# A norm at each layer boundary: rows shared by two engines, transposes in another order, a reciprocal root in nine steps, and memsets by words

## The reference

```python
def _layernorm(x, axis=-1, eps=1e-05):
    m = jnp.mean(x, axis=axis, keepdims=True)
    v = jnp.var(x, axis=axis, keepdims=True)
    return (x - m) / jnp.sqrt(v + eps)
...
x = x + _L0_xattn_ref(ctx_1024, _layernorm(x, axis=-1), ...)
x = x + _L0_ffn_ref(_layernorm(x, axis=-1), ...)
x = x + _L1_xattn_ref(_layernorm(x, axis=-1), ctx_1024, ...)
x = x + _L1_ffn_ref(_layernorm(x, axis=-1), ...)
x = x + _L2_xattn_ref(_layernorm(x, axis=-1), ctx_1024, ...)
x = x + _L2_ffn_ref(_layernorm(x, axis=-1), ...)
x = x + _L3_xattn_ref(_layernorm(x, axis=-1), ctx_1024, ...)
x = x + _L3_ffn_ref(_layernorm(x, axis=-1), ...)
```

## Time and profile before

| what | value |
| --- | --- |
| median of 3 runs | 2140.48 us (2140.2 to 2141.39) |
| the profiled execution's own time | 2137.22 us |
| its span in the profile | 2135.4 us |
| PE busy | 1727.2 us (81% of the span) |
| DVE busy | 1149.1 us (54%) |
| ACT busy | 731.7 us (34%) |
| POOL busy | 205.8 us (10%) |
| chain that ended last, by engine | PE 66%, DVE 20%, issue 6%, ACT 6% |

### The profile page before, as it was taken

One profiled execution on the slowest core, in us unless ns is written; L12 is line 12 of the kernel. 1 busy time (PEld: TensorE's weight loads), 2 busy tenths in 40 slices (PEclk: granted clock), 3 DMA queues, 4 the chain that ended last, 5 costly groups with the idle time before them and its releaser, 6 DMA issues.

```text
span 2135.4 us, 26508 instructions
## 1 busy us (share of the span) xinstructions
PE 1727.2 (81%) x8160; PEld 1137.7 (53%) x8160; DVE 1149.1 (54%) x2224; ACT 731.7 (34%) x1757; POOL 205.8 (10%) x307
## 2 busy tenths in 40 slices
PE   3565897478883558898879999997799999969998
PEld 1122654133332235675566555554688888756554
DVE  6898456664426857457453433434255544643444
ACT  3453212455552315335332111111465555512100
POOL 2222001000000002201200000000322222100000
PEclk7788898688987679999999999998799999969999
DMA  1000101000000010000010010000000000000000
GB/s 33 0 0 0 67 1 57 0 1 0 0 0 0 3 55 1 25 25 0 0 59 1 30 59 29 29 30 10 16 16 15 20 20 20 5 33 15 29 33 30
DMA packets 12118, 40.94 MB, mean 19 GB/s; under 512 B 2392, under 2 KB 5280, under 8 KB 9888
## 3 DMA queue, kind: packets, MB, share of 16 engines
q1 hardware_dynamic: 12064, 40.23, 5.4%
HBM read 39.18 MB, written 1.05 MB: 19 GB/s over the span
## 4 chain that ended last, share of the span: by engine, by line
PE 66%; DVE 20%; issue 6%; ACT 6%; POOL 1%; DVEq 1%; DMA 0%; ACTq 0%; SPq 0%; POOLq 0%
PE psum L1581 10%; PE psum L1597 5%; PE psum L2082 4%; DVE roomA L461 3%; PE psum L2091 3%; PE psum L1759 3%; PE psum L626 3%; PE psum L1762 3%; PE psum L1433 3%; PE psum L1827 3%; PE psum L1379 3%; DVE roomB L1015 2%; PE psum L1800 2%; PE psum L779 2%; PE psum L1778 2%
## 5 line engine op out<-in xcount | busy, mean ns | idle before, releaser
L1581 PE MATMUL psum<-own,roomB 128*128 128x512 f32 x512 | 232.4, 597 | 0.0
L1581 PEld LDWEIGHTS psum<-own,roomB 128*128 128x128 f32 x512 | 98.1, 192 | 96.6 <-issue 93.2
L1632 DVE SCALAR_TENSOR_TENSOR roomA<-psum,roomA 128x512 f32<-128x512 f32 x64 | 44.2, 691 | 184.7 <-PE psum L1581 171.1
L1618 ACT ACTIVATE roomA<-psum 128x512 f32<-128x512 f32 x64 | 38.2, 597 | 287.0 <-PE psum L1581 287.0
L1597 PE MATMUL psum<-roomB,roomA 128*128 128x256 f32 x512 | 121.1, 379 | 0.9 <-DVE roomA L1637 0.9
L1597 PEld LDWEIGHTS psum<-roomB,roomA 128*128 128x128 f32 x512 | 97.2, 190 | 41.4 <-issue 30.2
L1015 DVE TENSOR_REDUCE roomB<-psum 128x4 f32<-128x1024 f32 x64 | 78.4, 1226 | 71.4 <-PE psum L789 71.4
L339 PE MATMUL psum<-roomA,own 128*128 128x512 f32 x128 | 74.9, 716 | 36.7 <-POOL roomA L503 36.6
L1865 ACT ACTIVATE roomA<-psum,roomA 128x256 f32<-128x256 f32 x128 | 60.3, 484 | 86.7 <-DVE roomA L1924 86.7
L2082 PE MATMUL psum<-roomA,roomB 128*128 128x512 f32 (+1 forms) x192 | 86.6, 601 | 0.4 <-DVE roomA L2185 0.4
L919 ACT ACTIVATE roomA<-psum 128x1024 f32<-128x1024 f32 x64 | 65.7, 1026 | 54.8 <-PE psum L802 54.8
(11 more groups left out here) (361 smaller groups left out, 3628.5 us busy)
## 6 DMA issues: line engine op xcount, KB each, us to landing
roomB<-m_w_dram SPq DMA_DIRECT2D x8, 1536.0 KB, 6.4
roomB<-f_w_dram SPq DMA_DIRECT2D x8, 752.0 KB, 4.2
roomB<-a_w_dram SPq DMA_DIRECT2D x4, 1280.0 KB, 6.2
roomB<-a_qkv_dram SPq DMA_DIRECT2D x16, 256.0 KB, 2.6
roomB<-f_up_dram SPq DMA_DIRECT2D x2, 1152.0 KB, 6.7
roomB<-a_o_dram SPq DMA_DIRECT2D x8, 256.0 KB, 2.6
roomB<-f_down_dram SPq DMA_DIRECT2D x1, 1152.0 KB, 10.1
own<-x_dram SPq DMA_DIRECT2D x2, 512.0 KB, 4.3
```

What stands on the lines that cost most here:

```text
L1581: ins = pe.matmul(g.bank(4 + 2 * (u % 2) + w), parts(q)[0][:, kt, c:c + P], g.XT[:, kt, half * HALF:(half + 1) * HALF], start=(kt == 0), s ...
```

## The change

The norm is rewritten. The reciprocal root is `rsqrt_two`: the same first guess, then one step of a higher order and one Newton step, 9 instructions in place of 11. For a layernorm one more small instruction writes `-mean * rstd` (`g.t8b`), which ACT needs as a bias. DVE writes only the first 5 tiles, ACT writes the last 3 (`ACT.Identity` with scale and bias per partition, or `ACT.Copy` with a scale for the root-mean-square kind). The banks are ordered by tokens, so that banks 0 and 1 need tiles 1 to 4 and banks 2 and 3 the rest. ACT copies banks 0 and 2, DVE banks 1 and 3. In `mamba` DVE keeps all 8 tiles (`alone=True`). In `attn1` POOL's two memsets write 4-byte words, half as many elements.

```diff
-def rsqrt_steps(dve, step, out, v, t1, t2, eps, src=None):
-    step(dve.tensor_scalar(v, v if src is None else src, eps, None, ALU.add))
-    step(dve.tensor_scalar(out.bitcast(I32), v.bitcast(I32), -0.5, float(0x5F3759DF), ALU.mult, ALU.add))
-    for _ in range(3):
-        step(dve.tensor_tensor(t1, out, out, ALU.mult))
-        step(dve.scalar_tensor_tensor(t2, t1, -0.5, v, ALU.mult, ALU.mult))
-        step(dve.scalar_tensor_tensor(out, t2, 1.5, out, ALU.add, ALU.mult))
...
+def rsqrt_two(dve, step, out, v, t1, t2, eps, src):
+    K = 3 / 8
+    step(dve.tensor_scalar(v, src, eps, None, ALU.add))
+    step(dve.tensor_scalar(out.bitcast(I32), v.bitcast(I32), -0.5, float(0x5F3759DF), ALU.mult, ALU.add))
+    step(dve.tensor_tensor(t1, out, out, ALU.mult))
+    step(dve.tensor_tensor(t2, t1, v, ALU.mult))
+    step(dve.scalar_tensor_tensor(t1, t2, -10 / 3, t2, ALU.add, ALU.mult))
+    step(dve.scalar_tensor_tensor(out, t1, 5.0, out, ALU.add, ALU.mult))
+    step(dve.tensor_tensor(t1, out, out, ALU.mult))
+    step(dve.scalar_tensor_tensor(t2, t1, -0.5 * K ** 3, v, ALU.mult, ALU.mult))
+    return dve.scalar_tensor_tensor(out, t2, 1.5 * K, out, ALU.add, ALU.mult)
...
+    OWN = NT if alone else 5
...
-        for i in range(NT):
+        ins = rsqrt_two(dve, step, g.rstd, g.var, g.t8a, g.t8b, eps, g.var if rms else var)
+        if rms or alone:
+            ins.then_inc(s["norm_rstd"], 1)
+            dve.wait_ge(s["norm_rstd"], n + 1)
+        else:
+            step(ins)
+            dve.scalar_tensor_tensor(g.t8b, mean, -1.0, g.rstd, ALU.mult, ALU.mult).then_inc(s["norm_rstd"], 1)
+        for i in range(OWN):
...
-        dve.wait_ge(s["norm_ready"], NT * (n + 1))
+        if transposed:
+            for k in (1, 3):
+                dve.wait_ge(s["xt_psum"], 4 * g_tr + k + 1)
...
+                    ins = dve.tensor_copy(xt, g.bank(k))
...
+                    ins = dve.tensor_scalar(xt, g.bank(k), gain[:, k % 2:k % 2 + 1], None, ALU.mult)
+                ins.then_inc(s["xt_ready"], 1)
+        dve.wait_ge(s["norm_ready"], own0 + OWN)
+        dve.wait_ge(s["norm_tail"], tail0 + NT - OWN)
...
     def tensor(pe):
-        for bank in range(4):
-            kt, t0 = bank // 2, 4 * (bank % 2)
-            pe.wait_ge(s["norm_ready"], NT * n + t0 + 4)
+        for k in range(4):
+            kt, t0 = k % 2, 4 * (k // 2)
+            pe.wait_ge(s["norm_ready"], own0 + (4 if t0 == 0 else OWN))
+            if t0:
+                pe.wait_ge(s["norm_tail"], tail0 + NT - OWN)
...
     def scalar(act):
-        for bank in range(4):
-            act.wait_ge(s["xt_psum"], 4 * g_tr + bank + 1)
...
+        act.wait_ge(s["norm_rstd"], n + 1)
+        for i in range(OWN, NT):
+            if rms:
+                ins = act.activation(dst[:, i, :], src[:, i, :], ACT.Copy, scale=g.rstd[:, i:i + 1])
             else:
+                ins = act.activation(dst[:, i, :], src[:, i, :], ACT.Identity, scale=g.rstd[:, i:i + 1], bias=g.t8b[:, i:i + 1])
+            ins.then_inc(s["norm_tail"], 1)
+        if transposed:
+            for k in (0, 2):
+                act.wait_ge(s["xt_psum"], 4 * g_tr + k + 1)
...
-    gate_norm = norm(g, transposed=False)[0]["vector"]
+    gate_norm = norm(g, transposed=False, alone=True)["vector"]
...
-        pool.memset(aug[0][:, :, :, PARTS * HD:], 0.0).then_inc(s["a1_ones"], 1)
-        pool.memset(aug[1][:, :, :, PARTS * HD:], 1.0).then_inc(s["a1_ones"], 1)
+        pair_of_ones = 1.0 + 0x3F80 * 2.0 ** -23
+        for a, pair in ((aug[0], 0.0), (aug[1], pair_of_ones)):
+            words = a.rearrange("p t h c -> p (t h c)").bitcast(F32).rearrange("p (t h c) -> p t h c", t=NT, h=H)
+            pool.memset(words[:, :, :, PARTS * HD // 2:], pair).then_inc(s["a1_ones"], 1)
```

More of the change, by code:

```diff
@@ L196, in recycle, with norm @@
     return [dict(gpsimd=gpsimd)] + [{name: lambda eng: eng.wait_ge(s["recycled"], 1)} for name in ENGINES]
-def norm(g, transposed=True, src=None, dst=None, rms=False, gain=None):
+def rsqrt_two(dve, step, out, v, t1, t2, eps, src):
[9 more added lines that the diff above has]
+    return dve.scalar_tensor_tensor(out, t2, 1.5 * K, out, ALU.add, ALU.mult)
+def norm(g, transposed=True, src=None, dst=None, rms=False, gain=None, alone=False):
     s, n = g.sem, g.n_norm
@@ L206, in norm @@
     dst = g.XN if dst is None else dst
+    OWN = NT if alone else 5
+    own0, tail0 = g.n_own, g.n_tail
+    g.n_own += OWN
+    g.n_tail += NT - OWN
+    g_tr = g.n_xt
+    eps = 1e-5
     def vector(dve):
@@ L217, in vector @@
         step(ins)
+        mean, var = g.mv[:, :, 0], g.mv[:, :, 1]
         if rms:
-            step(dve.tensor_tensor(g.t8a, g.mv[:, :, 0], g.mv[:, :, 0], ALU.mult))
-            step(dve.tensor_tensor(g.var, g.mv[:, :, 1], g.t8a, ALU.add))
-        rsqrt_steps(dve, step, g.rstd, g.var, g.t8a, g.t8b, 1e-5, src=None if rms else g.mv[:, :, 1])
-        for i in range(NT):
+            step(dve.tensor_tensor(g.t8a, mean, mean, ALU.mult))
+            step(dve.tensor_tensor(g.var, var, g.t8a, ALU.add))
+        ins = rsqrt_two(dve, step, g.rstd, g.var, g.t8a, g.t8b, eps, g.var if rms else var)
[6 more added lines that the diff above has]
+        for i in range(OWN):
             if rms:
@@ L225, in vector @@
             else:
-                ins = dve.tensor_scalar(dst[:, i, :], src[:, i, :], g.mv[:, i, 0:1], g.rstd[:, i:i + 1],
+                ins = dve.tensor_scalar(dst[:, i, :], src[:, i, :], mean[:, i:i + 1], g.rstd[:, i:i + 1],
                                         ALU.subtract, ALU.mult)
             ins.then_inc(s["norm_ready"], 1)
-        dve.wait_ge(s["norm_ready"], NT * (n + 1))
-    def tensor(pe):
-        for bank in range(4):
-            kt, t0 = bank // 2, 4 * (bank % 2)
-            pe.wait_ge(s["norm_ready"], NT * n + t0 + 4)
+        if transposed:
+            for k in (1, 3):
+                dve.wait_ge(s["xt_psum"], 4 * g_tr + k + 1)
+                xt = xt_at(k)
+                if gain is None:
+                    ins = dve.tensor_copy(xt, g.bank(k))
+                else:
+                    ins = dve.tensor_scalar(xt, g.bank(k), gain[:, k % 2:k % 2 + 1], None, ALU.mult)
+                ins.then_inc(s["xt_ready"], 1)
@@ L235, in tensor, with xt_at @@
+        dve.wait_ge(s["norm_ready"], own0 + OWN)
+        dve.wait_ge(s["norm_tail"], tail0 + NT - OWN)
+    def xt_at(k):
+        return g.XT[:, k % 2, (k // 2) * HALF:(k // 2 + 1) * HALF]
+    def tensor(pe):
+        for k in range(4):
[3 more added lines that the diff above has]
+                pe.wait_ge(s["norm_tail"], tail0 + NT - OWN)
             for t in range(4):
-                ins = pe.transpose(g.bank(bank)[:, t * P:(t + 1) * P], dst[:, t0 + t, kt * P:(kt + 1) * P], g.ident)
+                ins = pe.transpose(g.bank(k)[:, t * P:(t + 1) * P], dst[:, t0 + t, kt * P:(kt + 1) * P], g.ident)
@@ new lines, in scalar @@
+        for i in range(OWN, NT):
+            if rms:
+                ins = act.activation(dst[:, i, :], src[:, i, :], ACT.Copy, scale=g.rstd[:, i:i + 1])
+            else:
+                ins = act.activation(dst[:, i, :], src[:, i, :], ACT.Identity, scale=g.rstd[:, i:i + 1], bias=g.t8b[:, i:i + 1])
[3 more added lines that the diff above has]
+                act.wait_ge(s["xt_psum"], 4 * g_tr + k + 1)
+                if gain is None:
+                    ins = act.copy(xt_at(k), g.bank(k))
+                else:
+                    ins = act.activation(xt_at(k), g.bank(k), ACT.Copy, scale=gain[:, k % 2:k % 2 + 1])
+                ins.then_inc(s["xt_ready"], 1)
@@ L249, in norm @@
+    if alone:
+        return dict(vector=vector)
     if not transposed:
-        return [dict(vector=vector)]
-    g_tr = g.n_xt
+        return [dict(vector=vector, scalar=scalar)]
     g.n_xt += 1
@@ L2236, in program @@
         g = Bundle()
[L2237 removed]
+        g.nc, g.d, g.n_norm, g.n_xt, g.n_own, g.n_tail = nc, d, 0, 0, 0, 0
         g.sem = Semaphores(lambda name: ctx.enter_context(nc.semaphore(name)))
```

6 lines of the change are left out of this document (removed).

## The result

| | before | after |
| --- | --- | --- |
| median of the runs | 2140.34 us (2138.03 to 2141.39, n 4) | 2124.39 us (2124.26 to 2128.39, n 4) |
| ratio after / before | | 0.9931, 95% interval 0.9914 to 0.9949 |
| profiled execution | 2137.22 us, span 2135.4 | 2124.31 us, span 2122.6 |
| PE / DVE / ACT busy | 1727.2 / 1149.1 / 731.7 us | 1721.7 / 1145.0 / 736.4 us |

Faster, by 12.9 us between the two profiled executions and 16.0 by the medians. The interval of the ratio leaves out 1.

What follows compares the result with a forecast made beforehand. It took the chain through the norm at each layer's head as the bound. Head terms summed to 6.4 us saved: 2137.22 to 2130.8 profiled, plus 3.3 to the median, 2134.1 us, range 2130.0 to 2138.5.

Steps and rivals of the forecast that it cites:

- the heads: Norms at the layers' starts, up to the first instruction needing them: 6.4 us saved in sum.
- The memset by words: In attn1, DVE is held off by POOL's memsets; half the elements would save 3.24 us.
- the whole of attn1: Head of attn1: memset, plain-head gain and hidden table load together save 3.50 us.
- attn2: Head of attn2: ACT's tiles stand behind its projections, so 1.30 us lost, bounds 0.8 and 2.3.
- moe3 and attn3's second norm: Root-mean-square heads: two steps fewer, 0.40, and a shorter pause, 0.05, save 0.45 us each.
- Plain heads: Layernorm heads such as attn4 and ffn5: 0.20 from steps, 0.31 from banks, 0.10 lost; 0.41 us saved each.
- ffn0: Head of ffn0: a transfer that does not move lets through 0 to 0.36 us; 0.10 taken.
- work in the turns keeps its order and pauses, so its pattern should move along whole: Attn1's turns: argument against an unkinder PE clock there, which would give 2141.6 us; that rival's chance 0.06.
- The rival of the kinder clock: Attn1's turns: PE's low granted clock rises from 0.81 to 0.93, 3 us taken, giving 2131; chance 0.12.
- POOL by bytes: Attn1's memsets cost by bytes, so attn1 keeps 0.26 us and the time is 2137.3; chance 0.07.
- the smaller heads: Heads of ffn1, attn3, ffn0 and attn2 give less than their terms: 2136.2 us; chance 0.10.
- The step to the median: Whole kernel: the median stands 3.3 us above the profiled execution, taking 2130.8 to 2134.1.

Runs made afterwards that it cites:

- b_root: The kernel before with the shorter reciprocal root alone; 2130.61 us, ratio 0.9968 to the kernel before.
- a_d8: The changed kernel with eight more small DVE steps, 1.6 us, at the end of mamba; 2125.29 us, ratio 0.9930 to the kernel before.
- a_slow9: The changed kernel with two more DVE steps, 0.4 us, in the norm at ffn5's head; 2125.69 us, ratio 0.9940 to the kernel before.

## Why the prediction was wrong

The forecast of the median was 9.7 us too high. Of these the heads are 0.9, what lies outside them 5.5, and the step from the profiled execution to the median 3.3.

- **The heads: right.** 7.26 against 6.4. The memset by words was worth 3.23 against 3.24, and the whole of attn1 3.80 against 3.50 (the prediction's own sum, 356.4 + 1.4 + 0.3, is 358.1 and not 358.14, so 3.54). ffn1 1.15 against 1.20: the reduction waits 0.18 for ACT's last tile. ACT's tile took 0.59 to 0.60 where 0.57 was priced, three 1.57 to 1.59 where 1.5 was. attn2 lost 0.86 and not 1.30: from the start of ACT's tiles to the energies it took 736.02 - 732.45 = 3.57, close to the 3.4 worked out, but ACT got there 0.6 sooner after the statistics, since PE's projections ahead of it took 5.58 instead of 6.21.
- **Small terms.** In moe3 and attn3's second norm 0.32 and about 0.20 came instead of 0.45: DVE's scaling copy from PSUM took 0.75, where 0.69 was assumed. Plain heads gave 0.58 instead of 0.41: the transposes gained 0.37 instead of 0.31, and DVE's tiles start 0.09 behind the bias step (1880.52, 1880.61), for which DVE does not wait, where a full step of 0.20 was counted. ffn0 gave 0.35, close to the upper bound, not 0.10.
- **What failed** is the step that set everything outside the heads to zero: "work in the turns keeps its order and pauses, so its pattern should move along whole". It does not move along whole: the same instructions run at another granted clock. Of 5.5 us, 5.1 came in attn2 (clock 1.00 instead of 0.79) and 3.3 in ffn5 (two falls instead of four), with 2.1 lost in moe3 and 2.2 in ffn0, and the others small. For attn1 alone, of which the sentence was written, it held: 0.29. The layers behind attn1 had no such term, and no reason was given for leaving it out. The rival of the kinder clock had the right kind, at 0.12, but looked for it in attn1's turns, where the rest changed by 0.29, and priced it at 3. POOL by bytes and the smaller heads did not come true.
- **The step to the median** was the second miss. The prediction put the median 3.3 above the profiled execution for both kernels. After the change both are equal (2124.31, 2124.39). The kernel before varies more: in the 31 runs beside `b_root` from 2125.58 to 2141.57, in batches with medians from 2136.2 to 2140.48. Added to 2137.22, the sum would have said 2130.8.
- **The two rules.** The sine ran 0.26 from 358.50, right when its angles were ready, 0.99 behind the table load's end at 357.51; in the kernel before it had started at 361.35, 0.01 behind the load's end. A drain of 1.38 us behind the load, which the Trainium skill, ScalarE: Activation LUTs, "What ACT_TABLE_LOAD costs", states, did not show in either. The 0.40 us that follows from the Trainium skill, VectorE: DVE Perf Modes, "The TRN2 errata", for an ACT pass of 256 elements was too low for one with two operands per partition: it took 0.59, near the 0.57 from the rows.

What is the change worth, then? The heads' 7.3 us are its own. The rest is a draw: with two steps added to every norm in both kernels the difference of the medians was 2.7 us (4.7 by the ratios), with them in ffn5 alone 6.1 (9.0), without them 14 to 16 (14 to 15). That the rest is PE's clock is shown for attn2 and ffn5 and, in its first 10 us, for moe3; for the other layers it was not looked into. What stays open is why a shift of 0.2 to 0.4 us decides, and why some executions draw otherwise in the same program; the runs show the dependence and not its mechanism.

## What to carry to other kernels

Price a change at its path first, then ask which short pauses of PE lie downstream at full clock: each may or may not cost a fall, so a range for a long program with such pauses must be several microseconds wider than its terms, on both sides. Judge an edit by its own stretch in two profiles, and by siblings shifted by a few tenths, not by the total alone; an added delay that makes the kernel faster is the sign of it. Tuning a head's length is no lasting gain, since the next edit can undo it. A better cure may be to close the pause of 0.8 us in front of the loop's matmuls; that was not tried.

## What was new about the hardware

- PE's granted clock can fall 0.5 to 0.7 us behind the end of a pause as short as 0.76 to 0.80 us. In the changed kernel, four such pauses were followed by the same eight matmuls in 2.00, 1.99, 3.15 and 3.24 us. The Trainium skill, TensorE: Matmul & The Clock Gate, "A second HAM failure mode: psum-queue depth-cycling", has PE idling briefly between groups of matmuls so often that its clock goes to and fro; by that, the trace agrees in kind, though the clock fell behind two of the five pauses of the loop here, four in the kernel before, and none in its second execution.
- The pattern is tied to the program in most executions, not in all. Three profiled executions of the changed kernel agree in ffn1 and every layer behind it within 0.1 us, and a shift of the later layers by 2.5 to 2.9 us (`a_d8`) changed none of them by more than 0.2. Yet the kernel before gave ffn5 in 251.23 and 247.47, and `a_slow9`, the same program as the changed kernel up to ffn5, gave attn2 in 44.33 instead of 39.14. The Trainium skill, TensorE: Matmul & The Clock Gate, Part 1, "What's actually happening", calls the warm-up run-variable; by that, the trace agrees for these two and for the layers ahead of ffn1 (ffn0 133.16, 133.14, 131.24), not for the three executions that agree.
- 0.4 us of DVE work at ffn5's head took 6.9 us out of that layer in the profiles (`b_slow9` against the first execution of the kernel before, 3.1 against the second), 1.0 us took 3.1 out of it in the changed kernel (`a_five9`).
- POOL's memset held a DVE step of 8 numbers for 3.4 to 4.0 us, and its price went by elements: 128x4096 halfwords 3.57, two of 128x2048 words 3.61 together.
